# Value mixing in column tiles and setup spread over the first tile, in a fused transformer block on one core

## What is computed

```python
x = x + xattn(layernorm(x), ctx)   # 16 heads of 64: softmax(q k^T / 8) v, concatenated, @ Wo + bo
x = x + tree(layernorm(x))         # 16 heads, causal, scores from sigmoid paths of depth 5
x = x + peer(layernorm(x))         # 8 heads, top 10 of 32 x 32 product keys, experts' down and up rows
# xattn:
q, k, v = heads(x @ Wq), heads(context @ Wk), heads(context @ Wv)
attn = softmax(einsum('bhid,bhjd->bhij', q, k) * scale)
out = einsum('bhij,bhjd->bhid', attn, v).transpose(0, 2, 1, 3).reshape(B, N, H * D) @ Wo + bo
```

## Time and profile before

| | |
|---|---|
| median of 3 runs | 1143.75 us (1143.23 to 1144.29) |
| the profiled execution | 1142.8 us |
| its span | 1141.0 us |
| mean granted clock of TensorE | 0.97 |
| PE busy | 1015.9 us, 89% |
| ACT busy | 960.2 us, 84% |
| DVE busy | 880.9 us, 77% |
| POOL busy | 824.6 us, 72% |

### The profile page before, as it was taken

The page is one execution under the profiler, slowest core; times in us unless marked ns, Lnnn a source line. Parts: engine busy times, 40 slices in busy tenths (PEclk is TensorE's granted clock), DMA queues, the critical chain, the costliest instruction groups (busy, mean ns, idle before and its releaser), DMA issues.

```text
span 1141.0 us, 34446 instructions
## 1 busy us (share of the span) xinstructions
PE 1015.9 (89%) x11656; PEld 769.5 (67%) x11656; DVE 880.9 (77%) x2929; ACT 960.2 (84%) x2252; POOL 824.6 (72%) x871
## 2 busy tenths in 40 slices
PE   3588999999999999999999999999999999999755
PEld 2466777766677777766776777667777776677433
DVE  1427788888888888888888888888888888888763
ACT  1558899999999989999999999999899899998652
POOL 0234777887777777987777778877777788777755
PEclk9899899999999999999999999999999999999875
DMA  5000000000000000000000000000000000000000
GB/s 142 24 13 14 4 14 16 16 14 16 16 12 8 16 16 16 16 14 16 16 4 16 16 16 16 14 16 16 5 15 16 16 16 14 14 13 7 4 3 5
DMA packets 36683, 18.78 MB, mean 16 GB/s; under 512 B 13632, under 2 KB 36256, under 8 KB 36512
## 3 DMA queue, kind: packets, MB, share of 16 engines
q1 hardware_dynamic: 36512, 16.58, 5.4%
HBM read 14.47 MB, written 2.10 MB: 15 GB/s over the span
## 4 chain that ended last, share of the span: by engine, by line
POOL 35%; DVE 21%; issue 14%; ACT 14%; PE 14%; SPq 1%; DMA 1%; POOLq 1%; DVEq 0%; ACTq 0%
POOL wsum L1038 23%; ACT p L649 7%; POOL feat L1022 5%; DVE cand L908 5%; DVE mw L937 4%; DVE best L913 3%; DVE best L903 3%; PE psXT L330 3%; ACT ew L737 3%; PE psXT L414 3%; POOL rstd L976 3%; ACT am L686 2%; PE psF L533 2%; POOL cand L1007 2%; SPq L230 1%
## 5 line engine op out<-in xcount | busy, mean ns | idle before, releaser
L1038 POOL TENSOR_TENSOR wsum<-wsum,mw 128x1024 f32<-128x1024 f32 x192 | 451.8, 2353 | 165.6 <-DVE mw L937 160.0
L937 DVE SCALAR_TENSOR_TENSOR mw<-psF,cut,ew 128x1024 f32<-128x1024 f32 x256 | 326.1, 1281 | 61.9 <-ACT ew L737 58.6
L737 ACT ACTIVATE ew<-psF,lnz 128x1024 f32<-128x1024 f32 x256 | 288.3, 1127 | 14.5 <-PE psF L533 11.3
L649 ACT ACTIVATE p<-psXT,negmax 128x128 f32<-128x128 f32 x512 | 182.2, 387 | 2.6 <-DVE negmax L810 2.5
L533 PE MATMUL psF<-sel,usT 128*128 128x512 f16 x512 | 158.6, 393 | 24.7 <-DVE mw L937 21.8
L330 PE MATMUL psXT<-cT,q 96*128 96x128 f32 x1024 | 141.0, 281 | 22.9 <-ACT p L649 18.5
L330 PEld LDWEIGHTS psXT<-cT,q 96*128 96x128 f32 x1024 | 129.1, 195 | 43.5 <-ACT p L649 35.3
L989 POOL TENSOR_TENSOR p<-p,rrow 128x512 f32<-128x512 f32 x128 | 131.5, 1038 | 16.9 <-DVE rrow L819 16.8
L365 PE MATMUL psXT<-pT,c 128*96 128x512 f32 x256 | 135.4, 612 | 0.0
L380 PE MATMUL psXT<-vo,uT 96*128 96x128 f32 x1024 | 121.2, 277 | 0.0
L649 ACT ACTIVATION_READ_ACCUMULATOR p<-psXT,negmax 128x1 f32 x512 | 117.2, 229 | 0.0
(11 more groups left out here) (137 smaller groups left out, 2266.1 us busy)
## 6 DMA issues: line engine op xcount, KB each, us to landing
cT<-cT_dram SPq DMA_DIRECT2D x32, 96.0 KB, 2.0
c<-c_dram SPq DMA_DIRECT2D x32, 96.0 KB, 2.1
x<-x_dram SPq DMA_DIRECT2D x32, 64.0 KB, 2.1
xr<-x_dram SPq DMA_DIRECT2D x32, 64.0 KB, 1.8
y_dram<-y SPq DMA_DIRECT2D x32, 64.0 KB, 2.1
wqT<-wqT_dram SPq DMA_DIRECT2D x1, 512.0 KB, 4.1
wo<-wo_dram SPq DMA_DIRECT2D x1, 512.0 KB
wdT<-wdT_dram SPq DMA_DIRECT2D x1, 512.0 KB
```

The source lines that it names most:

```text
L649: ins = act.activation(p[:, k, i, :], bank[BANK[f"x.s{k}"]][:, i * M:i * M + M], ACT.Exp, bias=negmax[:, k, i:i + 1], accum_out=rowsum[:, ...
L737: done(f"e.x{h}", act.activation(ew[:, h % NEW, :], bank[BANK[f"e.s{h}"]], ACT.Exp, bias=lnz[:, t % 4, h:h + 1]))
L937: done(f"e.w{h}", dve.scalar_tensor_tensor(out=mw[:, h % NMW, :], in0=bank[BANK[f"e.s{h}"]], scalar=cut[:, t % 4, h:h + 1], in1=ew[:, h % ...
L1038: done(f"e.a{h}", pool.tensor_tensor(wsum[:, t % 2, :], mw[:, 0, :] if h == 1 else wsum[:, t % 2, :], mw[:, h % NMW, :], ALU.add))
```

## The change

The mixing: for each y.m, the 96 context features are cut into three column tiles of 32, and a fourth column tile of the array is used as well. The eight heads are two groups of four. The first three heads of a group stay on rows 0 to 95 of the result (three column tiles, 384 columns). The fourth head's three parts of 32 features go to rows 96 to 127, below heads 0, 1 and 2 (128 columns each). Four heads then fill three blocks of 128 rows. `uT` and `vo` are laid out to fit, y.u copies 128 x 384, and y.out has 12 products over 128 rows.

The setup: the loads are spread over SP's and ACT's queues, x first. `qk` is split by ACT and DVE straight from PSUM. The products for `vo` run once ahead of x.s2 of tile 0, those of the keys ahead of x.p0, their copies ahead of x.e2 and x.t0 on ACT. On DVE the biases `bo` and `bp` are split ahead of x.x2, and the keys, their bias and `wd` ahead of y.res. Steps of tile 0 that need these parts get a wait.

```diff
-                    done(f"y.m{k}", pe.matmul(bank[BANK[f"y.m{k}"]][0:CD, :], c0[:, t % 2, k // 2, :], pT[:, k, :],
-                                              start=True, stop=True))
+                    probs = pT[:, k, :].rearrange("m (g j q) -> m g j q", g=2, j=4)
+                    to = bank[BANK[f"y.m{k}"]][:, 0:6 * N].rearrange("c (g j q) -> c g j q", g=2, j=3)
+                    for j in range(3):
+                        cols = c0[:, t % 2, k // 2, 32 * j:32 * j + 32]
+                        pe.matmul(to[32 * j:32 * j + 32], cols, probs[:, :, 0:3, :], start=True, stop=True,
+                                  tile_position=(0, 32 * j))
+                        mm = pe.matmul(to[96:128, :, j, :], cols, probs[:, :, 3, :], start=True, stop=True,
+                                       tile_position=(0, 96))
+                    done(f"y.m{k}", mm)
...
-                for h in range(XH):
-                    mm = pe.matmul(out, uT[:, h, :, :].rearrange("c b q -> c (b q)"), vo[:, h, :],
-                                   start=False, stop=(h == XH - 1))
+                for i in range(XH3):
+                    mm = pe.matmul(out, uT[:, i, :, :].rearrange("c b q -> c (b q)"), vo[:, i, :],
+                                   start=False, stop=(i == XH3 - 1))
...
-            for i, (dst, src) in enumerate(WEIGHTS):
-                sp.dma_start(dst if isinstance(dst, bass.AP) else dst[:], src)\
-                    .then_inc(own["wqk_load" if i < 2 else "wload"], 16)
-            run(steps, SP_ORDER)
+            load_x(0)
+            sp.dma_start(wqT[:], by_chunk(a["wqT"])).then_inc(own["wqk_load"], 16)
+            sp.dma_start(ident[:], a["ident"]).then_inc(own["wqk_load"], 16)
+            load_ct(0)
+            load_c(0)
+            load_xr(0)
...
+            def setup_vo():
+                pe.wait_ge(own["wvo_load"], 16 * 2)
+                pe.wait_ge(own["qk_split"], 4)
+                for j in range(4):
+                    if j >= 2:
+                        pe.wait_ge(own["setup_sb"], j + 3)
+
+                    for i in range(3):
+                        h, at = 4 * j + i, psF[:, i % 2 + 2 * (j % 2), (i // 2) * D:(i // 2 + 1) * D]
+                        r = XD * (h % 2)
+                        pe.matmul(at[0:CD], wvT[r:r + XD, h // 2, :], wo[r:r + XD, h // 2, :], start=True, stop=True)
+                    for i in range(3):
+                        h, at = 4 * j + 3, psF[:, i % 2 + 2 * (j % 2), (i // 2) * D:(i // 2 + 1) * D]
+                        mm = pe.matmul(at[CD:128], wvT[XD:2 * XD, h // 2, 32 * i:32 * i + 32], wo[XD:2 * XD, h // 2, :],
+                                       start=True, stop=True, tile_position=(XD, CD))
+                    mm.then_inc(own["setup_ps"], 1)
...
+            act.dma_start(wkT[:], by_chunk(a["wkT"])).then_inc(own["wqk_load"], 16)
+            act.dma_start(wvT[:], by_chunk(a["wvT"])).then_inc(own["wvo_load"], 16)
+            act.dma_start(wo[:], by_chunk(a["wo"])).then_inc(own["wvo_load"], 16)
+            act.dma_start(fwqT[:], by_chunk(a["fwqT"])).then_inc(own["key_load"], 16)
+            act.dma_start(fbqT[:], a["fbqT"]).then_inc(own["key_load"], 16)
+            act.dma_start(keys[:], a["keys"]).then_inc(own["key_load"], 16)
+            act.preload_act_table_set("natural_log_exp_and_others")
...
+            def setup_keys():
+                dve.wait_ge(own["setup_sb"], 9)
+                dve.tensor_tensor(fqk16[:, 1], psF[:, 0, :], fqk16[:, 0], ALU.subtract).then_inc(own["key_sb"], 1)
+                dve.wait_ge(own["key_sb"], 2)
+                parts(slice(0, 512), 1)
+                dve.wait_ge(own["expert_load"], 16 * 3)
+                dve.tensor_copy(wd16[:, 0], wdT[:]).then_inc(own["parts_done"], 1)
+                dve.wait_ge(own["parts_done"], 13)
+                dve.tensor_tensor(wd16[:, 1], wdT[:], wd16[:, 0], ALU.subtract).then_inc(own["split_done"], 1)
...
+            steps["x.stats"](0)
+            for j in range(4):
+                dve.wait_ge(own["setup_sb"], j + 1)
+                for e in range(2):
+                    lo, hi = (qk16[:, i, 4 * j + e:4 * j + 4:2, :] for i in (1, 0))
+                    ins = dve.scalar_tensor_tensor(out=lo, in0=pairs(j, CD, D)[:, e], scalar=QKSCALE, in1=hi,
+                                                   op0=ALU.mult, op1=ALU.subtract)
+                ins.then_inc(own["qk_split"], 1)
+            run(steps, DVE_ORDER, begun=("x.stats",), once={DVE_BIAS: setup_bias, DVE_KEYS: setup_keys})
...
+PE_VO = "x.s2"
+PE_KEYS = "x.p0"
+ACT_VO = "x.e2"
+ACT_KEYS = "x.t0"
+DVE_BIAS = "x.x2"
+DVE_KEYS = "y.res"
```

More of the change, by code:

```diff
@@ L126, in build, with by_chunk @@
         s = {n: sem(n.replace(".", "_")) for n in names}
-        own = {n: sem(n) for n in """wqk_load wload ones_set setup_ps setup_sb high_set split_done pool_set
+        own = {n: sem(n) for n in """wqk_load wvo_load key_load bias_load tree_load expert_load ones_set pool_set
+            setup_ps setup_sb qk_split key_sb parts_done split_done
             dve_path dve_tnorm dve_top dve_split dve_cand dve_zsum pool_inner pool_feat""".split()}
         block = ctx.enter_context(nc.Block())
[L131 to L141, removed]
+        def by_chunk(w):
+            return w.rearrange("(c p) d -> p c d", p=128)
         xt = a["x"].rearrange("(t p) d -> t p d", p=128)
@@ L153, in run @@
                 for name, lag in order.items():
-                    if 0 <= i - lag < NT:
-                        steps[name](i - lag)
+                    t = i - lag
+                    if t == 0 and name in once:
+                        once[name]()
+                    if 0 <= t < NT and not (t == 0 and name in begun):
+                        steps[name](t)
         def after(eng, name, t):
@@ L236, in _ @@
         def _(pe):
-            pe.wait_ge(own["wqk_load"], 16 * 2)
-            pe.wait_ge(own["ones_set"], 4)
[L240 to L262, removed]
+            def head_pairs(j, lw, rw, w, rows):
+                for i in range(4):
+                    h = 4 * j + i
+                    r = XD * (h % 2)
+                    mm = pe.matmul(psF[0:rows, h % 2 + 2 * (j % 2), (i // 2) * w:(i // 2 + 1) * w],
+                                   lw[r:r + XD, h // 2, :], rw[r:r + XD, h // 2, :], start=True, stop=True)
+                return mm
@@ new lines, in setup_keys @@
+            def setup_keys():
+                pe.wait_ge(own["key_load"], 16 * 3)
+                pe.wait_ge(own["setup_sb"], 8)
+                kflat = keys[:].rearrange("p g i -> p (g i)")
+                for c in range(2):
+                    mm = pe.matmul(psF[:, 0, 256 * c:256 * c + 256], fwqT[:, c, :], kflat, start=True, stop=True)
+                mm.then_inc(own["setup_ps"], 1)
+                for c in range(2):
+                    mm = pe.matmul(psF[0:96, 2, 256 * c:256 * c + 256], fbqT[:, c, :], kflat, start=True, stop=True)
+                mm.then_inc(own["setup_ps"], 1)
@@ L263, in _ @@
+            pe.wait_ge(own["wqk_load"], 16 * 3)
+            for j in range(4):
+                if j >= 2:
+                    pe.wait_ge(own["qk_split"], j - 1)
+                head_pairs(j, wqT, wkT, CD, D).then_inc(own["setup_ps"], 1)
+            pe.wait_ge(own["ones_set"], 4)
             pe.wait_ge(own["pool_set"], 3)
@@ L741, in _ @@
                 steps[f"e.x{h}"] = exp_sums(h)
-            run(steps, ACT_ORDER)
+            steps["x.norm"](0)
+            for j in range(4):
+                act.wait_ge(own["setup_ps"], j + 1)
+                act.activation(qk16[:, 0, 4 * j:4 * j + 4, :].rearrange("p (i e) c -> p e i c", e=2), pairs(j, CD, D),
+                               ACT.Copy, scale=QKSCALE).then_inc(own["setup_sb"], 1)
+            run(steps, ACT_ORDER, begun=("x.norm",), once={ACT_VO: setup_vo, ACT_KEYS: setup_keys})
         @block.vector
@@ new lines, in setup_bias, with setup_keys @@
+            def setup_bias():
+                dve.wait_ge(own["bias_load"], 16 * 2)
+                parts(slice(512, 720), 0)
+            def setup_keys():
+                dve.wait_ge(own["setup_sb"], 9)
[6 more added lines that the diff above has]
+                dve.tensor_tensor(wd16[:, 1], wdT[:], wd16[:, 0], ALU.subtract).then_inc(own["split_done"], 1)
```

112 lines of the change are left out of this document (72 added, 40 removed).

## The result

The changed kernel takes **1136.86 us** (median of 5 runs, 1135.89 to 1137.81), the kernel before 1143.75 beside it: a ratio of 0.9938, 95% interval 0.992 to 0.9956. It is faster, by 6.9 us and not by the forecast 18.7. The time lies within the forecast range. The profiled execution took 1135.89 us, its span is 1134.1.

The account below looks back on a forecast made before the run. Bound: a 32.41 us per-tile ring, two arms ending within 0.1 us. Start -25.9, value +5.0, keys +1.5, VectorE +2.5, y.out -1.8, ring 0: -18.7 from 1142.8 gives 1124.1, median 1125 us; range 1113 to 1184.

Parts of the forecast that it names:

- What bounds the kernel: Per-tile loop over all engines: two arms, POOL's and one behind the four y.m on PE, end within 0.1 us.
- y.out: Output projection cut from 16 to 12 products: 0.90 us less PE per tile, 1.8 us gained filling tiles 1 and 2.
- the ring: Repeating chain of dependent steps through the engines, one round per tile: 32.41 us, forecast to stay.
- y.m: Mixing in four overlapping column tiles on PE: 0.67 to 0.68 streaming plus 0.28 switching, 0.95 us, 0.05 more than now.
- The three rivals about the overlap (1.18, 1.85, 2.98): Mixing time in us: partial overlap 1.18, chance 0.25; starts in strict order 1.85, 0.09; no overlap 2.98, 0.09.
- D = 0.05 gives zero, the ring stays at 32.4 us: Steady loop: one mixing step growing by D = 0.05 us fits in the slack, so the period does not grow.
- The formula: Period growth per tile is 4D - 0.25 us, or zero, D being the growth of one mixing step.
- So the start moves by 39.2 - 13.3 = 25.9 us: Setup in parts: the first q product on PE comes at 13.3 instead of 39.2 us, 25.9 earlier.
- Value products, 5.0: Value-output products moved ahead of x.s2 in tile 0: four rounds on PE with copies, costing 5.0 us.
- VectorE's key part, 2.5: Splits of keys, biases and wd ahead of y.res of tile 0: 6.0 us of work, delaying y.res by 2.5.
- Key products, 1.5: Key products moved ahead of x.p0 in tile 0, with ACT's two copies ahead of x.t0: costing 1.5 us.
- the setup does not move the start as far: Rival: loads slow each other, or value part and DVE's key part cost 12 us more together: 1137 us, chance 0.07.

Follow-up runs that it names:

- the mixing alone: The kernel before with only the new mixing and the output projection of 12 products, its setup still in front of everything: 1150.89 us, ratio 1.0066.
- the first run: The changed kernel with the load of x of tile 1 issued right behind the four loads of tile 0: 1131.36 us, ratio 0.9892.
- 12, 128 and five counts without it: Empty VectorE instructions: 12 in the kernel before, 1147.74 us; 128 in the changed kernel, 1140.62 us; on time: the kernel before unpadded, the changed kernel with 116, 76, 8, 2.
- 76 more: The changed kernel with 76 empty instructions added to VectorE's list behind the bias part of tile 0: 1136.42 us.
- 2 more: The changed kernel with 2 empty instructions added to VectorE's list behind the bias part of tile 0: 1137.43 us, one execution.

## Why the prediction was right or wrong

- **What bounds the kernel: right.** Two arms within 0.1 us of each other, the second one behind the four y.m. The stall showed the slack: 0.25 late gave 0.15, so it was 0.1.
- **y.out: its length right, its place in the filling not.** 2.73 us, and nothing in the ring. The 1.8 us for tiles 1 and 2 are there in the table, but hardly by y.out: from y.res of tile 0 to the GELU of tile 1 it is 58.7 us in the kernel before, 58.5 with the mixing alone, 56.8 in the changed kernel, each with 3.4 us at the lower clock. The shorter y.out gave 0.9 us at tile 0 where the setup stands in front, and 0.2 behind. That the number came out is luck; what made the 1.8 is open.
- **y.m: right, with the parts of the sum otherwise.** 0.95 forecast; measured 0.79 plus 0.11 at the entry, 0.90. The streams were as reckoned (0.67), the entry and exit 0.23 and not 0.28. The three rivals about the overlap (1.18, 1.85, 2.98) are refuted: the three column tiles of 384 start within 0.03 us, and the fourth tile's six passes follow each other at 0.11 beside them, as reckoned. The rule weighed there (the Trainium skill, TensorE: Matmul & The Clock Gate, Part 3) says that matmuls start and end strictly in program order. The trace does not agree for the starts: in the program the short product of the second column tile (L404) stands ahead of the third tile's 384 columns (L402), but all three tiles of 384 have started by 596.52, and the second short pass starts at 596.63. A pass that waits on its own tile didn't hold up the others: twelve passes that would stream 2.7 us one after the other take 0.79.
- **"D = 0.05 gives zero, the ring stays at 32.4 us": the conclusion failed, not for D.** The formula stands (2.64 more gave 2.68, once the slack was gone). What was missing is a term that isn't in the steady work at all: 12 instructions more in VectorE's setup moved its loop against a place modulo 128, and 0.25 us fell on the division, between two steps of the ring. From the GELU of tile 1 to the last the changed kernel lost 2.9 us in the profiled executions.
- **"So the start moves by 39.2 - 13.3 = 25.9 us": this step failed, and it is the miss.** Each of its terms was about right (last split 14.1 for 12.8). What I left out was an order: ahead of x.low of tile 0 VectorE runs x.stats of tile 1, whose load stands last on SP. I had priced SP's 30 loads at 27 us and asked only whether t.pv waits for them. The true 17.2 instead of 25.9 is 8.7 us; with the load moved up, 24.3. Shown by the first run.
- **Value products, 5.0: 6.2.** I counted 8 passes a round; the third head doesn't run beside the fourth's parts, so it is 10 (1.09) and 0.28 more, which I put down to two switches of tiling; the first round ran mostly at half rate and took 2.07. The shortfall is small, but I never set it against the old part, which is 2.5: the mixing's cost of 3.7 us in the filling was booked under the setup. That hid that the first half of the change is worth nothing, or less.
- **VectorE's key part, 2.5: 2.8, plus a clock.** The idle time I wanted for it was there, but ahead of x.low of tile 1 and not behind it. Moving it there, together with the clock that then stays up, gave 5.6 us.
- **Key products, 1.5: 0.1.** Between x.s2 and y.out of tile 0 the changed kernel lost 0.1 us; this term was too high.
- **The sum with what was measured:** -17.2 + 6.3 + 0.1 + 2.8 - 1.8 + 2.9 = -6.9, where the forecast had -25.9 + 5.0 + 1.5 + 2.5 - 1.8 + 0 = -18.7.
- **The rival "the setup does not move the start as far", 1137,** gave the time almost exactly, by another mechanism than the ones it named: luck. It had 0.07. (In the sum of the chances for "faster" the 0.05 of "more gain than I count" is missing.)

What stays open: what the stall at VectorE's record 63 is. That the division's delay is bound to the place modulo 128 is shown, by 12, 128 and five counts without it. Not every instruction at that place is late: with 76 more it is one of the maxima of k.cand, which waits for no semaphore, and starts on time; with 2 more it is a reciprocal that waits, and starts 0.12 us later than usual.

## What to carry to other kernels

When setup is moved behind the first steps, follow every engine's list from the first useful step backwards, with the lags: what stands ahead of it may belong to the next tile, and hang on a transfer that nobody thought urgent. Price a change of layout where the layout is made, too, against the old way of making it. And in a ring with a slack of 0.1 us a period that moved by 0.15 may have nothing to do with the edit: compare the records that start with nothing to wait for ("issue") in both traces, and shift one engine's program by a few empty instructions before a mechanism is believed.

## What the runs showed of the hardware

- Twelve passes of f32 in four column tiles over all 128 rows, two passes of 384 columns and then two of 128 in program order, hold PE for 0.79 us; one after the other they would stream 2.7 (6 x 0.337 + 6 x 0.113). The first passes of the four tiles start within 0.03 us, and those of the later tiles don't wait for the short passes that stand ahead of them in the program.
- VectorE's division behind a semaphore wait started 0.25 us late in all seven traces in which it is record 63 modulo 128 of its engine, and on time in all nine others. A reciprocal with a wait at that place was 0.12 us late, a maximum without one not at all.
- An empty VectorE instruction with a satisfied wait takes 0.072 us.
- The same value products ran at 0.21 us a pass behind 12.66 us of idle PE, and at 0.109 behind work, with 1.00 in the granted clock's column both times. The traces hold no record of the clock before 36.4 us (mixing alone) and 27.5 us (changed kernel, just where its passes go from 0.21 to 0.11), and without a record the column shows 1.00. So it doesn't show which of the two levels holds at the start; the passes' spacing does.
- Between y.res of tile 0 and the first GELU, TensorE's clock at 1.2 instead of 2.4 GHz for 13.7 us went with 4.0 to 4.6 us more time, for 10.2 us with 2.4 to 2.5, against 25.7 us with none.
